# Top-1 experts: the second product as three terms from split parts, run one tile behind the first product, with gathers issued one tile further ahead of the scatters

## What is computed

```
ms = mean(x*x); xn = x * rsqrt(ms + EPS) * rms_w
top1_idx = argmax(softmax(xn @ gate_w.T)); top1_score = max(...)
for e in range(8):
    h  = silu(xn @ W1[e] + b1[e])          # 256 -> 1024
    ye = h @ W2[e] + b2[e]                 # 1024 -> 256
    out = where(top1_idx == e, ye, out)
return out * top1_score
```

## Time and profile before

| | us |
|---|---|
| median of three runs | 1043.21 |
| lowest, highest | 1036.62, 1043.94 |
| the profiled execution | 1039.09 |
| its span | 1037.2 |
| the tile loop in it, from the first record of first(0) to the end of second(22) | 299.8 to 468.5 |
| TensorE busy over the span | 933.0 (90%) |
| ScalarE, VectorE, GpSimd busy | 501.0, 613.8, 307.8 |

### The profile page before, as it was taken

One profiled execution on the slowest core, in us unless ns is written; L12 is line 12 of the kernel. 1 busy time (PEld: TensorE's weight loads), 2 busy tenths in 40 slices (PEclk: granted clock), 3 DMA queues, 4 the chain that ended last, 5 costly groups with the idle time before them and its releaser, 6 DMA issues. The chain is left out here.

```text
span 1037.2 us, 17297 instructions
## 1 busy us (share of the span) xinstructions
PE 933.0 (90%) x6786; PEld 639.6 (62%) x6786; DVE 613.8 (59%) x1054; ACT 501.0 (48%) x753; POOL 307.8 (30%) x295
## 2 busy tenths in 40 slices
PE   3389999999989999998589989999989899999993
PEld 3134444445669999997434444444479889999993
DVE  7688989996521111104687858787726455565553
ACT  1148887776142323233247856766611044555550
POOL 6696761000012322212404031000003345444222
PEclk9559999999799999998869999999988989999997
DMA  7877665301599999976625251600107125544316
GB/s 264 171 213 192 142 156 107 47 3 64 191 360 423 351 340 333 347 261 151 189 52 137 42 115 34 125 4 4 63 22 245 41 68 159 153 129 123 102 21 183
DMA packets 53046, 158.97 MB, mean 153 GB/s; under 512 B 8273, under 2 KB 28369, under 8 KB 42289
## 3 DMA queue, kind: packets, MB, share of 16 engines
q1 hardware_dynamic: 36464, 121.96, 39.6%
q0 software_dynamic: 13296, 29.63, 10.9%
q10 hardware_dynamic: 3216, 6.43, 1.7%
HBM read 116.18 MB, written 40.76 MB: 151 GB/s over the span
## 5 line engine op out<-in xcount | busy, mean ns | idle before, releaser
L927 DVE TENSOR_REDUCE a_row_max<-ps_ring 128x2 f32<-128x1024 f32 x256 | 308.4, 1221 | 66.6 <-PE ps_ring L690 63.9
L853 ACT ACTIVATE a_probs<-ps_ring 128x1024 f32<-128x1024 f32 x256 | 261.1, 1023 | 96.8 <-PE ps_ring L705 94.3
L724 PE MATMUL ps_out<-a_probs,a_vaug 128*32 128x256 f32 x2048 | 165.2, 395 | 1.5 <-ACT a_out_sb L859 1.0
L690 PE MATMUL ps_ring<-a_ka,a_qa 52*128 52x512 f32 (+1 forms) x512 | 123.6, 485 | 38.1 <-DMA a_ka<-scratch_k_scr 19.8
L705 PE MATMUL ps_ring<-a_qa,a_ka 56*128 56x512 f32 (+1 forms) x512 | 130.5, 506 | 1.4 <-DVE a_row_max L927 1.3
L1196 ACT ACTIVATE e_hid<-ps_ring,e_wts 128x128 f32<-128x128 f32 x184 | 52.0, 370 | 114.8 <-DMA e_wts<-in_w 58.9
L705 PEld LDWEIGHTS ps_ring<-a_qa,a_ka 56*128 56x128 f32 (+1 forms) x512 | 48.6, 186 | 93.8 <-issue 65.5
L1542 ACT ACTIVATE e_hr<-ps_ring 128x512 fp32r<-128x512 f32 x64 | 38.3, 598 | 124.2 <-PE ps_ring L1597 80.6
L690 PEld LDWEIGHTS ps_ring<-a_ka,a_qa 52*128 52x128 f32 (+1 forms) x512 | 52.1, 201 | 74.0 <-DVE a_row_max L927 24.1
L1597 PE MATMUL ps_ring<-e_xt,e_wr 128*128 128x512 f32 x384 | 91.6, 399 | 2.9 <-DVE e_xt L1658 2.9
L724 PEld LDWEIGHTS ps_out<-a_probs,a_vaug 128*32 128x32 f32 x2048 | 40.8, 108 | 75.9 <-issue 73.4
(11 more groups left out here) (240 smaller groups left out, 1251.5 us busy)
## 6 DMA issues: line engine op xcount, KB each, us to landing
e_wts<-in_w SPq DMA_DIRECT2D x23, 1156.0 KB
e_wts<-in_w SPq DMA_DIRECT2D x23, 1024.0 KB
e_wf<-in_w SPq DMA_DIRECT2D x16, 1024.0 KB, 6.8
a_qa<-scratch_q_scr SPq DMA_DIRECT2D x28, 384.0 KB, 8.7
a_ka<-scratch_k_scr SPq DMA_DIRECT2D x28, 384.0 KB, 7.1
scratch_q_scr<-a_qst POOLq DMA_DIRECT2D x36, 256.0 KB, 3.6
scratch_k_scr<-a_kst POOLq DMA_DIRECT2D x9, 512.0 KB, 12.7
scratch_q_scr<-a_qst SPq DMA_DIRECT2D x12, 256.0 KB, 3.2
```

Source lines behind the costliest of these rows:

```text
L690: ins = pe.matmul(to[:, par], qa[rows, b % 2, g, p, qt * P:(qt + 1) * P], ka[rows, b % 2, g, p], start=True, stop=True)
L724: ins = pe.matmul(m.ps_out[VW * h:VW * (h + 1), cols], vaug[:, b % NV, kc, HG * g + h], probs[:, t % 3, h, cols], start=(kc == 0 and half ...
L853: nc.scalar.activation(probs[:, t % 3, 2 * half:2 * half + 2], unit("s", n), ACT.Exp, scale=HD ** -0.5).then_inc(exp_done, 1)
L927: dve.tensor_reduce(row_max[:, s % 3, qt, :, p], unit("m", n), AX.X, ALU.max).then_inc(mx_read, 1)
```

## The change

- `turns` writes out the first two turns and loops over the rest.
- New tensors: `hid_parts` (high and low part of `hid`, two tiles), `bias2` (a copy of b2, two tiles), and `w2_parts`, the high and low part of W2 for two tiles. `w2_parts` has no memory of its own: it lies on `kst`.
- ScalarE gets two copies per tile: `second_high` (W2 of the tile, 128 x 2048, rounded to float32r) at the head of the tile and the rounding of `hid` (128 x 1024) behind its SiLU pieces. For tile 0 `second_high` stands last and waits until all key stores have landed (`m.k_stored`). The wait that SyncE had for them at the end is gone.
- VectorE gets three instructions per tile: a copy of b2, and the subtractions that leave the low parts of W2 (`second_low`) and of `hid`. The addition of b2 now belongs to the tile before.
- second(n) is 24 float32r products (high x high, low x high, high x low, eight chunks each). On TensorE it stands behind first(n+1) and turn(n+2).
- SyncE issues w2(n) when W2 of tile n-2 is split and its SiLU is done.
- GpSimd issues the gather of tile n+3 ahead of the scatter of tile n.

```diff
 def turns(eng, n, body):
     body(0)
-    with eng.Fori(1, n) as it:
+    body(1)
+    with eng.Fori(2, n) as it:
...
+        hid_parts = sb("hid_parts", [P, 2, 2, FC, P], F32R)
+        bias2 = sb("bias2", [P, 2, D], F32)
+        w2_parts = kst[:].rearrange("p b r c t -> p (b r c t)").rearrange("p (k r f) -> p k r f", k=2, r=2)
...
-                        wait_from(sp, y_copied, n - 1)
+                        wait_from(sp, w2_split, n - 1)
+                        wait_from(sp, hid_ready, 8 * n - 8)
...
-                sp.wait_ge(m.k_stored, 48 * B)
...
+                gather(2)
                 for n in range(n_tiles):
-                    gather(n + 2)
+                    gather(n + 3)
                     pool.wait_ge(y_copied, n + 1)
...
+                def second_high(k):
+                    nc.scalar.copy(w2_parts[:, k, 0], wts[:, k, w1_cols:w1_cols + FC * D]).then_inc(w2_high, 1)
+
                 def turn_of_loop(it, ks=range(2)):
                     for k in ks:
                         n = it * 2 + k
                         act.wait_ge(w2_in[k], 16 * it + 16)
                         wait_from(act, y_full, n - 1)
+                        if not isinstance(n, int) or n:
+                            second_high(k)
+                        wait_from(act, hid_split, n - 1)
...
+                        act.wait_ge(hid_ready, 8 * n + 8)
+                        nc.scalar.copy(hid_parts[:, k, 0], hid[:, k]).then_inc(hid_high, 1)
+                        if isinstance(n, int) and n == 0:
+                            act.wait_ge(m.k_stored, 48 * B)
+                            second_high(k)
...
+                terms = ((0, 0), (1, 0), (0, 1))
+                def second(n, k):
+                    pe.wait_ge(hid_split, n + 1)
+                    pe.wait_ge(w2_split, n + 1)
+                    wait_from(pe, y_copied, n - 1)
+                    for fc in range(FC):
+                        for hp, wp in terms:
+                            ins = pe.matmul(m.ps_max[:, k, 0:D], hid_parts[:, k, hp, fc], w2_parts[:, k, wp, fc * D:(fc + 1) * D],
+                                            start=(fc == 0 and (hp, wp) == (0, 0)), stop=(fc == FC - 1 and (hp, wp) == (0, 1)))
+                    ins.then_inc(y_full, 1)
...
-                        pe.wait_ge(w2_in[k], 16 * it + 16)
-                        wait_from(pe, y_copied, n - 1)
-                        for fc in range(FC):
-                            if fc % 4 == 0:
-                                pe.wait_ge(hid_ready, 8 * n + 4 + fc)
-                            ins = pe.matmul(m.ps_max[:, k, 0:D], hid[:, k, fc], wts[:, k, w1_cols + fc * D:w1_cols + (fc + 1) * D], start=(fc == 0), stop=(fc == FC - 1))
-                        ins.then_inc(y_full, 1)
+                        if not isinstance(n, int) or n:
+                            second(n - 1, 1 - k)
...
                 turn_of_loop(n_tiles // 2, range(1))
+                second(n_tiles - 1, 0)
                 keep_awake(16)
...
+                def second_low(n, k):
+                    dve.wait_ge(w2_high, n + 1)
+                    wait_from(dve, y_copied, n - 1)
+                    dve.tensor_copy(bias2[:, k], wts[:, k, W0_COLS - D:W0_COLS])
+                    dve.tensor_tensor(w2_parts[:, k, 1], wts[:, k, w1_cols:w1_cols + FC * D], w2_parts[:, k, 0].bitcast(F32), ALU.subtract).then_inc(w2_split, 1)
+                def biased(n, k, stored):
+                    dve.wait_ge(y_full, n + 1)
+                    wait_from(dve, y_stored[k], 16 * stored)
+                    dve.tensor_tensor(ys[:, k], m.ps_max[:, k, 0:D], bias2[:, k], ALU.add).then_inc(y_copied, 1)
                 def turn_of_loop(it, ks=range(2)):
                     for k in ks:
                         n = it * 2 + k
+                        if not isinstance(n, int) or n:
+                            second_low(n, k)
                         if not isinstance(n, int) or n + 1 < n_tiles:
                             dve.wait_ge(xst_full, n + 2)
                             dve.tensor_tensor(xst[:, 1 - k], turned, weight.to_broadcast([P, DC, P]), ALU.mult).then_inc(xst_ready, 1)
-                        dve.wait_ge(y_full, n + 1)
-                        wait_from(dve, y_stored[k], 16 * it)
-                        dve.tensor_tensor(ys[:, k], m.ps_max[:, k, 0:D], wts[:, k, W0_COLS - D:W0_COLS], ALU.add).then_inc(y_copied, 1)
+                        dve.wait_ge(hid_high, n + 1)
+                        dve.tensor_tensor(hid_parts[:, k, 1], hid[:, k], hid_parts[:, k, 0].bitcast(F32), ALU.subtract).then_inc(hid_split, 1)
+                        if isinstance(n, int) and n == 0:
+                            second_low(n, k)
+                        else:
+                            biased(n - 1, 1 - k, it - 1 + k)
```

More of the change, by code:

```diff
@@ L1072, in moe_top1 @@
         hid_ready = sem("hid_ready")
+        hid_high = sem("hid_high")
+        hid_split = sem("hid_split")
+        w2_high = sem("w2_high")
+        w2_split = sem("w2_split")
         y_full = sem("y_full")
@@ L1369, in turn_of_loop @@
                             dve.tensor_tensor(xst[:, 1 - k], turned, weight.to_broadcast([P, DC, P]), ALU.mult).then_inc(xst_ready, 1)
-                        dve.wait_ge(y_full, n + 1)
-                        wait_from(dve, y_stored[k], 16 * it)
-                        dve.tensor_tensor(ys[:, k], m.ps_max[:, k, 0:D], wts[:, k, W0_COLS - D:W0_COLS], ALU.add).then_inc(y_copied, 1)
+                        dve.wait_ge(hid_high, n + 1)
[4 more added lines that the diff above has]
+                            biased(n - 1, 1 - k, it - 1 + k)
                 turns(dve, n_tiles // 2, turn_of_loop)
                 turn_of_loop(n_tiles // 2, range(1))
+                biased(n_tiles - 1, 0, n_tiles // 2)
 def moe_top_k(nc, m, dram):
```

## The result

Median 1052.58 us (1047.57 to 1058.25, 4 runs) against 1041.26 (4 runs): ratio 1.0125, 95% interval 1.0082 to 1.0169. Beside the first experiments the same kernel was measured again: 1.0192 (1.0143 to 1.0241). It is slower, by 1 to 2%; the forecast had 0.67 on staying within 1% and 0.27 on slower by more.

What follows compares the result with a forecast made beforehand. TensorE was taken to set the loop's pace, transfers close behind. Profiled: 1039.1 - 12.5 + 13.4 + 3.1 + 1.0 - 1.2 = 1042.9 us; on the median 1047.0, stated as 1046, range 1037 to 1056.

Steps and rivals of the forecast that it cites:

- The pace: In the tile loop, a tile costs 6.67 us instead of 7.24, saving 12.5 us over 22 tiles.
- The head: At the loop's start, W2's first split waits for key stores until 316.6 us; second(0) starts at 321.4: +13.4 us.
- the clock's price: After TensorE idles at the loop's start, products run at a granted clock of 0.50: +3.1 us (1.5 to 3.5).
- GpSimd's queue: In the loop, gathers behind scatters that wait for a later `ys` have 1.0 us less; nothing put in the sum.
- The window of 7.6 us: In the loop, time from a gather going out until its transposition wants it; 8.6 us before.
- At most 0.3 more: In the loop, extra time in us for a gather's issue beside VectorE's long subtraction.
- a margin of 0.1: In the loop, the us by which a gather's landing, taken at the scatter's median of 7.5, was covered at zero cost.
- Rival 2: In the loop, the gather's landing sets the pace: 10 us, or 5 with every second gather late; chance 0.10.
- The two rules: For the loop, the skill's 358 GB/s limit (some 6 us more) and VectorE copies locking GpSimd out (620 ns becomes 3100).
- rival 1: In the loop, the transfers set the pace at 6.9 to 7.1 us per tile: +2 to +12 us, chance 0.28.
- The tail: At the loop's end, second(22) needs 3.9 us after first(22), behind second(21) of 2.88: +1.0 us.
- The forecast's own range: For the whole kernel, without the rivals' widening: 1042 to 1052 us on the median's scale; chance 0.45.

Runs made afterwards that it cites:

- the first experiments: Group of edits to the changed kernel, measured with that kernel unchanged as their base; unchanged, it had ratio 1.0192 to the kernel before.

## Why the prediction held, and where it didn't

**The pace: right.** 6.67 forecast, 6.63 measured. Second products cost 2.9 as in the last layer. ScalarE's copies took 1.90 and 1.05, VectorE's instructions 0.29, 2.28 and 1.22: each within 0.05 of its estimate, and hidden. The run with the terms at the old place shows that the shift hides them.

**The head: right, slightly low.** The stores released ScalarE at 318.7, forecast 316.6 plus the 0.8 by which this loop began later; second(0) started at 323.3 (321.4 + 0.8). At full clock the cost is 14.5 us instead of 13.4, the clock's price 2.6 instead of 3.1, shown by the run that kept TensorE busy. But "the head costs 16 us" is not what own memory gives back. It gave 9 alone and 5 with the early gathers, since SyncE still held W2 of tile 2 until the first split, and `xst` of tile 3 stands behind the split of that W2 on VectorE. With tile 0 in the common order the head lost 1.2 us against the kernel before (31.2 for 30.0, first(0) to first(4)).

**GpSimd's queue: wrong, and the step that cost most.** The window of 7.6 us was right: 337.99 to 345.64. Its other side was not. "At most 0.3 more" for the issue was read from the earlier trace rows, where issues met subtractions of 512 and 1024 columns. Beside one of 2048 it took up to 3.05 instead of 0.97, 2.1 more, against a margin of 0.1. I put zero in the sum; the late tiles cost 7.0 of the loop's 7.3 us in one profile and 12.6 of the 12.7 in the other. Rival 2 (chance 0.10) had the place and a price of 5 to 10, but put it down to a slow landing and not to a held-up issue. It also had no price for the clock, which fell behind two of the twelve gaps of the two profiles, so that there a wait of 2.04 cost 3.8. The two rules stood the other way round than I weighed them. The Trainium skill (SBUF — State Buffer, "SBUF: two separate sides") has GpSimd locked out while VectorE holds a port pair that the two share. What I took from it was its case of a copy on VectorE; the instruction here was a subtraction, and the same section names an instruction with two SBUF inputs too, against a GpSimd one that reads SBUF. The lock-out is borne out: the issues ended 0.83 to 0.86 us after the subtraction.

**Transfers: rival 1 fell, by little.** With the gathers early the engines carried 382 GB/s and TensorE had no gap; but in the run with the subtraction in pieces TensorE waited 4.1 us for `xst` behind weights that came late. The Trainium skill's 358 GB/s (SBUF — State Buffer, "A bandwidth-pool intuition that's wrong") is exceeded, writes included, in that stretch.

**The tail**: 1.5 us of gap before second(22), forecast 1.0. **The sum** for the loop: +14.5 + 2.6 - 22 x 0.61 + 7.3 - 2.4 + 1.5 = +10.1, measured 178.9 - 168.7 = +10.2. The forecast had +3.8; the 7.3 is the missing term. The measured median of 1052.6 lies in the range of 1037 to 1056 only because rival 1, which did not come true, had widened it upwards: that is luck. The forecast's own range ended at 1052.

## What to carry to other kernels

When a step is moved later, follow every queue that waits for its result: here a gather "one tile further ahead" still stood behind a scatter whose data came one tile later. A price of two engines side by side must be read from an instruction as long as the new one. And memory borrowed from a buffer that is still being stored costs a wait where the borrower is first used, but freeing it pays only if the order of the transfers, and of the engines that prepare the next tile, lets the freed time be used.

## What the runs showed of the hardware that was not expected

- An indirect transfer's issue on GpSimd that begins during a VectorE subtraction with both inputs in SBUF (128 x 2048, 2.28 us) ends 0.83 to 0.86 us after that subtraction, wherever in it the issue began from 0.06 us on. Begun before it, or within 0.03 us of its start, it takes 0.97 to 1.06. In four pieces of 512 columns, the longest issue is 1.23.
- A gap of 2.04 us on TensorE, 370.76 to 372.80, was followed by a granted clock of 0.69 over 372 to 377 us, and one of 1.98 by 0.73 over 395 to 401. One of 1.91 in the other profile of the same kernel was followed by 1.00 over 452 to 457, and one of 2.38 in the run that kept TensorE busy in the head by 1.00 over 354 to 359. What sets them apart is not shown.
